# A graph network's node stage: state sums and the experts' first layer kept in PSUM, casts and low parts moved between engines

## The reference

```
m = relu(concat(h[src], edge_attr) @ W1.T + b1) @ W2.T + b2
agg = segment_sum(m, dst)
gi = agg @ W_ih.T + b_ih;  gh = h @ W_hh.T + b_hh       # h = layernorm(x)
r = sigmoid(i_r + h_r);  z = sigmoid(i_z + h_z);  n = tanh(i_n + r * h_n)
h_new = (1 - z) * n + z * h
x1 = x + h + gamma * (h_new - mean) * rsqrt(var + eps) + beta
g = layernorm(x1) @ Wg + bg;  two largest of 8, softmax of them -> comb
hidden = relu(layernorm(x1) @ W1[e] + b1[e]);  out = sum_e comb[e] * (hidden @ W2[e] + b2[e])
y = x1 + out + 0.5 * (relu(layernorm(x1) @ Ws1 + bs1) @ Ws2 + bs2)
```

## Time and profile before

| | |
|---|---|
| median of the runs (3) | 1444.93 us |
| the profiled execution's own time | 1446.94 us |
| its span, first to last instruction | 1445.1 us |
| mean granted TensorE clock | 0.990 |
| TensorE busy | 1367.7 us, 95% |
| VectorE busy | 1076.2 us, 74% |
| GpSimd busy | 909.6 us, 63% |
| ScalarE busy | 772.1 us, 53% |

### The profile page before, as it was taken

How to read it: one execution, slowest core, us unless ns; L and a number is a source line. 1 busy time by engine, 2 the same in 40 slices (tenths; PEclk the granted TensorE clock), 3 DMA queues, 4 the chain that set the end, 5 groups by cost and what they waited for, 6 DMA issues and landing times. The chain is left out here.

```text
span 1445.1 us, 22692 instructions
## 1 busy us (share of the span) xinstructions
PE 1367.7 (95%) x6398; PEld 1096.4 (76%) x6398; DVE 1076.2 (74%) x2428; ACT 772.1 (53%) x1586; POOL 909.6 (63%) x1042
## 2 busy tenths in 40 slices
PE   4889999999689999999999999999999999999996
PEld 3678888887577777777777777777777777778774
DVE  3586334233578888888888888888888888888886
ACT  3431322202556666666666666666666666666652
POOL 3211143105567887787787877777777777877771
PEclk9999999999889999999999999999999999999998
DMA  8222543255433333333333333333333333333330
GB/s 305 68 73 88 175 150 124 88 203 199 151 114 117 116 116 130 117 115 118 125 122 104 129 122 123 103 131 118 123 107 131 117 120 111 131 116 117 115 110 29
DMA packets 62863, 179.57 MB, mean 124 GB/s; under 512 B 9328, under 2 KB 9968, under 8 KB 62704
## 3 DMA queue, kind: packets, MB, share of 16 engines
q1 hardware_dynamic: 46912, 99.20, 20.0%
q0 software_dynamic: 15920, 79.97, 16.6%
HBM read 141.86 MB, written 37.29 MB: 124 GB/s over the span
## 5 line engine op out<-in xcount | busy, mean ns | idle before, releaser
L1528 PE MATMUL bank<-whh_hi,x_hi 128*128 128x512 f32 x948 | 381.6, 402 | 0.8 <-DVE whh_lo L883 0.7
L1528 PE MATMUL bank<-whh_hi,x_lo 128*128 128x512 f32 x948 | 375.1, 396 | 0.0
L1528 PE MATMUL bank<-whh_lo,x_hi 128*128 128x512 f32 x948 | 374.8, 395 | 0.0
L1528 PEld LDWEIGHTS bank<-whh_hi,x_lo 128*128 128x128 f32 x948 | 178.3, 188 | 42.9
L1528 PEld LDWEIGHTS bank<-whh_hi,x_hi 128*128 128x128 f32 x948 | 178.5, 188 | 40.4 <-issue 1.1
L1528 PEld LDWEIGHTS bank<-whh_lo,x_hi 128*128 128x128 f32 x948 | 178.6, 188 | 39.8
L1281 POOL DMA_INDIRECT gates<-gates_in,slot_at x79 | 115.2, 1459 | 64.6 <-POOL slot_at L1279 62.1
L1322 POOL TENSOR_TENSOR h_n<-h,n_gate 128x512 f32<-128x512 f32 x79 | 109.1, 1381 | 60.0 <-ACT n_gate L1394 60.0
L1307 POOL TENSOR_TENSOR hn<-hn_raw,hn_bias 128x512 f32<-128x512 f32 x79 | 106.2, 1344 | 56.5 <-ACT hn_raw L1363 55.6
L1335 POOL TENSOR_TENSOR x_h_b<-x_h,bn_shift 128x512 f32<-128x512 f32 x79 | 104.5, 1323 | 14.4 <-ACT x_h L506 9.1
L1312 POOL TENSOR_TENSOR r_hn<-r_gate,hn 128x512 f32<-128x512 f32 x79 | 102.9, 1303 | 12.7 <-ACT r_gate L1374 1.8
(11 more groups left out here) (183 smaller groups left out, 3276.0 us busy)
## 6 DMA issues: line engine op xcount, KB each, us to landing
xt<-in_x SPq DMA_DIRECT2D x79, 256.0 KB, 2.8
x_lo_raw<-in_x_cols SPq DMA_DIRECT2D x79, 256.0 KB, 2.6
out<-y SPq DMA_DIRECT2D x79, 256.0 KB, 2.8
gates_in<-g_out SPq DMA_DIRECT2D x16, 768.0 KB, 3.7
wih_lo_raw<-in_wih_t SPq DMA_DIRECT2D x4, 768.0 KB, 12.4
whh_rows<-in_whh SPq DMA_DIRECT2D x4, 768.0 KB, 5.8
whh_lo_raw<-in_whh_t SPq DMA_DIRECT2D x4, 768.0 KB, 7.9
gates_in<-late_out SPq DMA_DIRECT2D x6, 256.0 KB, 6.4
```

The source lines that it names most:

```text
L1528: last = pe.matmul(to[0:R, :], a[:, s, k * R:(k + 1) * R], w[:, k, q * D:(q + 1) * D], start=n == 0, stop=n == 3 * DK - 1)
```

## The change

`z_gate`, `z_h_n`, `h_new` and `scaled` no longer exist in SBUF: the sigmoid of z writes into z's own PSUM bank (`chain`), and the state operations work there in place. TensorE's first z product of a tile therefore waits for `x1` of the tile before. The bias sum `f1` is made in place in the bank of the experts' first layer; `comb1` and the numbers 0 to 7 (`experts`) lie in spare columns of that bank. TensorE's first layer waits for `hid` instead of `f1`.

n's part: `hn_raw` is gone; VectorE makes `hn` from the bank with scale and bias in one operation, after `r_pre`. ScalarE takes the cast of `extra` into `hid` and the shared relu, and `x_high` stands earlier on it. GpSimd takes `x_lo` and the low part of `extra`. Its order in a period: second norm, `x_h_b` (now of t+1), `x_lo`, slot copy, low part of `extra`, `r_hn`, `n_pre`, `h_n`, first norm, gather. VectorE makes the combination for t-1, after the statistics, and no longer for t-2 at the head of the period. `z_pre` now stands before `hid_lo`. The first two gathers no longer wait behind two `x_h_b`. A semaphore is merged into another one (`is_lo_step`). Cut to its core:

```diff
-    hn_raw = place("hn_raw", [R, 2, D])
...
-    z_gate = place("z_gate", [R, D])
...
-    z_h_n = place("z_h_n", [R, D])
-    h_new = place("h_new", [R, D])
-    scaled = place("scaled", [R, D])
...
-    f1 = place("f1", [R, F1])
...
-    comb1 = place("comb1", [R, NE])
...
+    chain = b_z[0:R, :]
+    f1 = b_f1[0:R, 0:F1]
+    spare = F1 + 8
+    experts = b_f1[0:R, spare:spare + NE]
+    comb1 = b_f1[0:R, spare + NE:spare + 2 * NE]
...
+            def slots(p, k):
 
                 s, t = p.slot(k), p.t
                 pool.tensor_copy(slot_at[:, s:s + 1], node_slot[:, bass.ds(t + k, 1)]).then_inc(slot_copied, 1)
...
+            def gather(p, k):
...
+                if p.first(1):
+
+                    pool.wait_ge(table_in, 16)
+                    slots(p, 1)
+                    slots(p, 2)
+                    pool.wait_ge(late_stored, 16 * 3 * SUP)
+                    gather(p, 1)
+                    gather(p, 2)
+                    for s in range(2):
+                        pool.memset(hid[:, s, HE + 3 * V:KF * P], 0.0).then_inc(hid_set, 1)
+                    pool.memset(extra[:, V - 1:V], 0.5).then_inc(hid_set, 1)
...
-                if p.has(0):
-                    s = p.slot(0)
-                    pool.wait_ge(hn_raw_done, t + 1)
-                    wait_from(pool, r_hn_done, t - 1)
-                    pool.tensor_tensor(hn[:, s, :], hn_raw[:, s, :], hn_bias[:, :], ALU.add).then_inc(hn_done, 1)
+                if p.has(1):
+                    s = p.slot(1)
+                    pool.wait_ge(x_h_done, t + 2)
+                    wait_from(pool, x1_done, t)
+                    pool.tensor_tensor(x_h_b[:, s, :], x_h[:, s, :], bn_shift[:, :], ALU.add).then_inc(x_h_b_done, 1)
+                if p.has(1) and not p.early(1):
+                    x_low(pool, p)
+                if p.has(2) and not p.early(2):
+                    pool.wait_ge(gates_loaded[p.slot(0)], 16 * (p.turn(0) + 1))
+                    slots(p, 2)
+                if p.has(-2):
+                    s = p.slot(-2)
+                    pool.wait_ge(extra_hi_done, t - 1)
+                    pool.tensor_tensor(hid[:, s, HE + 2 * V:HE + 3 * V], extra[:, :], hid[:, s, HE:HE + V],
+                                       ALU.subtract).then_inc(extra_lo_done, 1)
...
-                if p.has(0):
-                    s = p.slot(0)
...
-                    s = p.slot(2)
-                    pool.wait_ge(x_h_done, t + 3)
-                    wait_from(pool, x1_done, t + 1)
-                    pool.tensor_tensor(x_h_b[:, s, :], x_h[:, s, :], bn_shift[:, :], ALU.add).then_inc(x_h_b_done, 1)
-                if p.first(1):
-
-                    pool.wait_ge(g_prod, 3 * EC)
...
+                if p.has(1) and not p.early(1):
+                    x_high(act, p)
...
-                if p.has(0):
-                    s = p.slot(0)
-                    act.wait_ge(n_prod, t + 1)
-                    wait_from(act, hn_done, t - 1)
-                    act.wait_ge(rstd_done[1], t + 1)
-                    act.activation(hn_raw[:, s, :], b_n[0:R, :], ACT.Identity,
-                                   scale=rstd[1][:, p.slot4(0):p.slot4(0) + 1]).then_inc(hn_raw_done, 1)
...
+                if p.has(-2):
+                    s = p.slot(-2)
+                    act.wait_ge(comb_done, t - 1)
+                    wait_from(act, hid_turned, t - 3)
+                    act.activation(hid[:, s, HE:HE + 2 * V].bitcast(F32R).rearrange("p (q v) -> p q v", q=2),
+                                   extra[:, :].unsqueeze(1).broadcast_to((R, 2, V)), ACT.Copy).then_inc(extra_hi_done, 1)
+                if p.has(-1):
+                    act.wait_ge(h2_turned, t)
+                    wait_from(act, f1_prod, t - 1)
+                    act.activation(h2_hi[:, :], b_th2[:, 0:DK * R], ACT.Copy).then_inc(h2_hi_done, 1)
...
-                if p.has(1) and not p.early(1):
-                    x_high(act, p)
-                if p.has(-1):
-                    act.wait_ge(h2_turned, t)
-                    wait_from(act, f1_prod, t - 1)
-                    act.activation(h2_hi[:, :], b_th2[:, 0:DK * R], ACT.Copy).then_inc(h2_hi_done, 1)
...
-                    wait_from(act, z_h_n_done, t)
-                    act.activation(z_gate[:, :], z_pre[:, :], ACT.Sigmoid).then_inc(z_done, 1)
+                    act.activation(chain, z_pre[:, :], ACT.Sigmoid).then_inc(z_done, 1)
...
+                    act.wait_ge(top_i_done, t)
+                    wait_from(act, extra_lo_done, t - 1)
+                    act.activation(extra[:, 0:HS], f1[:, NE + HE:F1], ACT.Relu, scale=0.5).then_inc(shared_done, 1)
...
+            def products_of_n(dve, p):
+                s = p.slot(1)
+                dve.wait_ge(n_prod, p.t + 2)
+                wait_from(dve, r_hn_done, p.t)
+                dve.wait_ge(rstd_done[1], p.t + 2)
+                dve.scalar_tensor_tensor(hn[:, s, :], b_n[0:R, :], rstd[1][:, p.slot4(1):p.slot4(1) + 1],
+                                         hn_bias[:, :], ALU.mult, ALU.add).then_inc(hn_done, 1)
+
+            def first_products(dve, p):
+
+                dve.wait_ge(iotas, 9)
+                dve.wait_ge(g_added, 3 * EC)
+                dve.tensor_copy(experts, iota8[:, :]).then_inc(top_f_done, 1)
+                products_of_n(dve, p)
...
-                if p.has(-2):
...
-                    dve.tensor_scalar(comb1[:, :], iota8[:, :], top_f[:, 0:1], weight[:, 0:1], ALU.is_equal, ALU.mult)\
-                        .then_inc(comb1_done, 1)
...
-                    dve.tensor_tensor(extra[:, HS:HS + NE], comb1[:, :], comb2[:, :], ALU.add).then_inc(comb_done, 1)
-
-                    dve.tensor_scalar(extra[:, 0:HS], f1[:, NE + HE:F1], 0.0, 0.5, ALU.max, ALU.mult)\
-                        .then_inc(shared_done, 1)
...
-                    dve.tensor_copy(hid[:, s, HE:HE + 2 * V].bitcast(F32R).rearrange("p (q v) -> p q v", q=2),
-                                    extra[:, :].unsqueeze(1).broadcast_to((R, 2, V))).then_inc(extra_hi_done, 1)
-                    dve.wait_ge(extra_hi_done, t - 1)
-                    dve.tensor_tensor(hid[:, s, HE + 2 * V:HE + 3 * V], extra[:, :], hid[:, s, HE:HE + V],
-                                      ALU.subtract).then_inc(hid_done, 1)
...
-                if p.has(-2):
-                    dve.wait_ge(hid_hi_done, t - 1)
-                    dve.tensor_tensor(hid_lo[:, :], b_thid[:, 0:(KF - 1) * R],
-                                      hid_hi[:, 0:(KF - 1) * R].bitcast(F32), ALU.subtract)\
-                        .then_inc(hid_lo_done, 1)
-                if p.has(1) and not p.early(1):
-                    x_low(dve, p)
...
+                if p.has(-2):
+                    dve.wait_ge(hid_hi_done, t - 1)
+                    dve.tensor_tensor(hid_lo[:, :], b_thid[:, 0:(KF - 1) * R],
+                                      hid_hi[:, 0:(KF - 1) * R].bitcast(F32), ALU.subtract)\
+                        .then_inc(hid_lo_done, 1)
...
-                    dve.tensor_tensor(f1[:, :], b_f1[0:R, 0:F1], f1_bias[:, :], ALU.add).then_inc(f1_done, 1)
+                    dve.tensor_tensor(f1, f1, f1_bias[:, :], ALU.add).then_inc(f1_done, 1)
...
-                    dve.tensor_tensor(gap[:, :], top[:, 0:1], top[:, 1:2], ALU.subtract).then_inc(gap_done, 1)
+                    dve.tensor_scalar(gap[:, :], top[:, 0:1], top[:, 1:2], None, ALU.subtract).then_inc(gap_done, 1)
...
-                    dve.tensor_copy(top_f[:, :], top_i[:, 0:2]).then_inc(comb1_done, 1)
+                    dve.tensor_copy(top_f[:, :], top_i[:, 0:2]).then_inc(top_f_done, 1)
...
-                    dve.tensor_tensor(z_h_n[:, :], z_gate[:, :], h_n[:, :], ALU.mult).then_inc(z_h_n_done, 1)
+                    dve.tensor_tensor(chain, chain, h_n[:, :], ALU.mult).then_inc(z_h_n_done, 1)
...
-                    dve.tensor_tensor(h_new[:, :], z_h_n[:, :], n_gate[:, s, :], ALU.add).then_inc(h_new_done, 1)
+                    dve.tensor_tensor(chain, chain, n_gate[:, s, :], ALU.add).then_inc(h_new_done, 1)
...
-                    dve.tensor_tensor(scaled[:, :], h_new[:, :], bn_scale[:, :], ALU.mult).then_inc(scaled_done, 1)
+                    dve.tensor_tensor(chain, chain, bn_scale[:, :], ALU.mult).then_inc(scaled_done, 1)
...
-                    dve.tensor_tensor(x1[:, p.slot4(0), :], scaled[:, :], x_h_b[:, s, :], ALU.add).then_inc(x1_done, 1)
+                    dve.tensor_tensor(x1[:, p.slot4(0), :], chain, x_h_b[:, s, :], ALU.add).then_inc(x1_done, 1)
...
+                if p.has(-1):
+                    s = p.slot(-1)
+
+                    dve.wait_ge(weight_done, 2 * t)
+                    dve.wait_ge(top_f_done, t + 1)
+                    dve.tensor_scalar(comb1, experts, top_f[:, 0:1], weight[:, 0:1], ALU.is_equal, ALU.mult)\
+                        .then_inc(comb1_done, 1)
+                    dve.tensor_scalar(comb2[:, :], experts, top_f[:, 1:2], weight[:, 1:2], ALU.is_equal, ALU.mult)\
```

(44 more changed lines are left out.)

44 lines of the change are left out of this document (14 added, 30 removed).

## The result

| | before | after |
|---|---|---|
| median of the runs (4 and 4) | 1443.64 us | 1422.08 us |
| ratio, with 95% interval | | 0.9844 (0.9814 to 0.9875) |
| the profiled execution, and its span | 1446.94, 1445.1 us | 1422.28, 1420.5 us |
| VectorE, GpSimd busy | 1076.2, 909.6 us | 1030.6, 827.6 us |
| mean period of 76 starts | 13.17 us | 12.88 us |

A forecast was written before the change was run, and what follows sets the result against it. TensorE, 95% busy, was taken as the bound. From the profiled 1446.94 us, 23.3 in the loop and 1.7 at the start gave 1421.9, less 2.0 to the median 1420 us; forecast 1412 to 1427 (0.58), upper end 1441.

The forecast's parts named there:

- 12.83 is its floor: TensorE's loop period: an undisturbed one takes 12.83 us, so at most 0.34 a period, 25.5 us, can be won.
- Why hid is late, and that this stall goes: VectorE's hid product and the cast behind it wait for GpSimd, some 1.1 us each; the change removes TensorE's stall.
- GpSimd's ring: State chain, second norm and GpSimd's part through h_n, each waiting for the last: lengthened from 11.42 to 12.86 us.
- Where it touches TensorE, c = 1.15: TensorE waits once the state chain starts 1.15 us or more after the start of TensorE's next period.
- The added waits, ScalarE's casts: ScalarE's relu and cast of extra wait for VectorE work that is by then done: costed at nothing.
- PSUM in place, 0.69: VectorE's state operations in PSUM take 0.69 us each; bounds for the four together -0.04 and +0.24.
- The cast that stays: VectorE's top_f, right ahead of the state chain, may be held beside GpSimd's h_n: 0 to +0.1 on the ring.
- x_lo's type on GpSimd: x_lo's output type, so far written only by VectorE, brings no surcharge on GpSimd; bounds -0.1 and +0.5.
- The start, 1.7: Before the loop, the wait of 1.60 us for the first hid goes; with it 1.7 us are won.
- 1: Rival: GpSimd's ring sets the period above the floor, at 13.05 us, giving 1434 us; chance 0.22.
- 2: Rival: x_lo on GpSimd overfills the ring, to 13.35 us, giving a slower 1457 us; chance 0.10.
- 3: Rival: hid stays late, its low part waiting for ScalarE and GpSimd behind x_lo; period near 13.15, 1443 us; chance 0.10.

The follow-up runs named there:

- ring_short: The changed kernel with x_lo on GpSimd moved ahead of the second norm, into its wait for the statistics: 1388.57 us, ratio 0.961.
- short_scalar: `ring_short` plus one operation of hn_raw's size ahead of h2 on ScalarE, waiting for n's last product: 1405.82 us, ratio 0.9729.
- before_f1_psum: The kernel before with only the experts' bias sum f1 made in place in PSUM: 1427.73 us, ratio 0.9878.
- ring_long: The changed kernel with one more 41-column GpSimd operation between the slot copy and the low part of extra: 1439.4 us, ratio 0.9958.
- idle_long: The changed kernel with one more 41-column GpSimd operation behind the gather, where GpSimd waits for the statistics: 1420.87 us, ratio 0.9829.
- chain_sbuf: The changed kernel with z_gate, z_h_n, h_new and scaled back in SBUF, z waiting for z_pre: 1423.21 us, ratio 0.9847.
- cast_late: The changed kernel with VectorE's cast top_f behind the statistics instead of right ahead of the state chain: 1423.02 us, ratio 0.9843.

## Why the prediction was right, and where it was not

1420 was predicted, 1422.08 measured, by mostly the mechanism that was written down. That the sum comes so near is in part luck: predicted were 23.3 in the loop, 1.7 at the start and 0 at the end, 25.0 together; measured were 21.7, 4.0 and -1.1, 24.6 together. By its steps:

- *"12.83 is its floor"*: wrong. TensorE's own work takes 12.44. I had compared a disturbed period with an undisturbed one and called the latter free of waits, having looked at the matmuls' rows alone; the 0.52 <-ACT h stood on the weight load. Against the period of `ring_short` shown above (12.48), the one from 1000.68 to 1013.51 loses 0.22 + 0.06 around the turning of h (`short_scalar`: 0.24 a period in all) and 0.11 between the turning of hid and the first layer, and gains 0.04 between the two turnings: 0.35. The 0.11 lies where the first layer waits for h2's low part (there it ends at 1010.10, and the first layer starts at 1010.16); on ScalarE x_hi stood ahead of h2's high part until the change put it earlier. No run tried this alone. So the most that the loop could give was 0.73 x 75 = 55 us, not 25.5. The number of the prediction survived only because the ring, at 12.86, lay above both floors.
- *Why hid is late, and that this stall goes*: right. Hid's product is at 0.42 always, and `before_f1_psum` shows the cause.
- *GpSimd's ring*: right, term by term. Predicted and measured, from start to start: second norm 0.83, 0.80; x_h_b 1.24, 1.26; x_lo 1.24, 1.23; slot copy and low part 0.40, 0.38; r_hn 1.47, 1.44; n_pre 2.04, 2.03; h_n 1.38, 1.41; state chain and statistics with the step to GpSimd 4.26, 4.30. Sum 12.86, 12.85. `ring_long`, `idle_long` and `ring_short` show it from both sides.
- *Where it touches TensorE, c = 1.15*: mis-sized. c is 0.98 (997.77 - 996.79), and h2 is ready at c + 6.07 (1003.84) against 5.98. But the turning of h is due at 7.00, not 7.23, so TensorE waits from c = 0.93. Hid's turning is due at 7.00 + 0.35 + 1.50 = 8.85, not 9.12, while the low part ends at 1005.78, c + 8.01; and TensorE turns hid only 0.25 behind that end (0.24 to 0.26 in the loop), where it turns h 0.05 behind ScalarE's h2. I had put this step from GpSimd to TensorE at nothing. With it hid is the place that binds first, from c = 8.85 - 8.01 - 0.25 = 0.59; I had it at 1.15, with h at 1.25. TensorE loses 0.08 + 0.06 at h and 0.27 + 0.03 at hid.
- *The added waits, ScalarE's casts*: right at nothing. In the loop neither is among the waits of TensorE or GpSimd, and no relu or cast is in the ring. In three of the last tiles GpSimd's low part does wait for ScalarE's cast, 1.76, 1.09 and 8.21 us.
- *PSUM in place, 0.69*: 0.70; nothing either way, by `chain_sbuf` too. The estimate from the Trainium skill, VectorE: DVE Perf Modes, section "The TRN2 errata", 65 ns an operation and 1439 us, is not borne out by any row here.
- *The cast that stays*: it is held (1.09), as feared, but costs the ring nothing that `cast_late` could show; bounds 0 to +0.1, right at the lower.
- *x_lo's type on GpSimd*: no surcharge, 1.29.
- *The start, 1.7*: 4.0. TensorE before and after, its long waits ahead of the loop:

```profile
398.96 1.11 PE L525 MATMUL bank<-ident,h 128*128 128x128 f32 x4 [11.69 <-ACT h L1369]
```

```profile
395.52 0.79 PE L1547 MATMUL bank<-whh_hi,x_hi 128*128 128x512 f32 x1 [10.50 <-DVE x L1493]
```

z's first product now waits for x1 (an added wait that I priced in the loop, not here); it is met at 395.52, and z's first half, which stood ahead of the long wait before, now fills part of what was a wait for h2. So far this gains little: the turning of h starts at 398.64 instead of 398.96. The other 3.7 us come behind it, where TensorE's granted clock is higher. The view by stretches (length, busy time and instructions of PE, PEld, DVE, ACT and POOL, then granted clock, DMA share, GB/s), before and after:

```profile
400.00:405.00 5.00, 5.00 (x23) 4.28 (x22) 3.16 (x4) 1.86 (x3) 4.01 (x6) 0.71 0.26 77
...
415.00:421.00 6.00, 5.50 (x23) 4.82 (x24) 4.37 (x14) 2.55 (x6) 3.10 (x7) 0.72 0.25 87
```

```profile
400.00:405.00 5.00, 4.90 (x27) 4.00 (x26) 3.19 (x8) 1.71 (x6) 4.09 (x5) 1.00 0.35 108
...
415.00:421.00 6.00, 6.00 (x29) 4.92 (x28) 5.03 (x11) 3.51 (x9) 4.14 (x6) 1.00 0.17 57
```

  Before, the stretch behind the wait of 11.69 and the one behind hid's first wait of 1.60 lie between TensorE's two clock levels (1.2 and 2.4 GHz, here 0.50 and 1.00): 0.71 and 0.72. Now both are at 1.00: TensorE takes up work 3.4 us earlier ahead of the first, and there is no wait for hid ahead of the second. I had the wait in the sum and the clock only in the range. How the 3.7 divide between the hid wait and the clock was not tried.
- *The end, 0*: 1.1 us given back. Where it goes was not followed up.
- *From profile to median*: I took off 2.0 since the profiled execution of before lay that far above its median. The one of after lies at its median (1422.28, 1422.08). Without that step the sum, 1421.9, meets it.
- *Rivals*: Of 1 the mechanism came, but not the size: the ring does set the period above TensorE's own work, by 0.44, yet at 12.85 and not 13.05, since its unknown terms are nothing. 2 did not come (x_lo 1.29). Of 3 only the place was right: hid's turning now waits for GpSimd's low part, 0.27 in each period.

What I did not ask at all was what the change gives away. The ring "lengthened to TensorE's own floor" seemed free because the floor was read 0.39 too high; it costs 75 x 0.44 = 33 us.

## What to carry to other kernels

A period without a visible stall is not the engine's floor: add up its own work (distances between starts where nothing waits), read the weight-load rows as well as the matmuls', and see whether each handover starts as soon behind the last product as it ever does. Sum a ring term by term before moving work into it, and put work that no one in the ring needs into the idle time before the ring's wait: the same operation cost 17 us in the ring and nothing beside it. Moves can be worth something only together, and one of them can cost more than all of them win, so undo them one at a time before keeping them all.
